# A routed expert block on one core: gate weights centred once, logits from the residual, and the rows sent in two steps

## The reference

```
x1  = x + tanh(g_xattn) * attention(ctx, ctx, layernorm(x))      # one head, width 128, per sequence of 64
n   = layernorm(x1)
logits = n @ gate_w.T                                           # 8 experts
top 2 of softmax(logits)
out = x1 + tanh(g_ffn) * sum over the 2 experts of  p * (gelu(n @ w1[e].T + b1[e]) @ w2[e].T + b2[e])
```

## Time and profile before

| | |
|---|---|
| median of 3 runs | 113.01 us (112.81 to 113.17) |
| the profiled execution: its time | 113.34 us |
| its span, first to last instruction | 111.6 us |
| mean granted TensorE clock | 0.814 |
| PE, DVE, ACT, POOL busy | 72.3, 52.6, 50.1, 53.4 us |

### The profile page before, as it was taken

One profiled execution on the slowest core, in us unless ns is written; L12 is line 12 of the kernel. 1 busy time (PEld: TensorE's weight loads), 2 busy tenths in 40 slices (PEclk: granted clock), 3 DMA queues, 4 the chain that ended last, 5 costly groups with the idle time before them and its releaser, 6 DMA issues.

```text
span 111.6 us, 2488 instructions
## 1 busy us (share of the span) xinstructions
PE 72.3 (65%) x707; PEld 61.9 (55%) x707; DVE 52.6 (47%) x222; ACT 50.1 (45%) x155; POOL 53.4 (48%) x79
## 2 busy tenths in 40 slices
PE   5667955774664200570599999999999999920000
PEld 2256823554454200210399999999999999910000
DVE  1377855499978728309812332433134213310261
ACT  4122387689676600600056654754577277600000
POOL 6668501133677777760000547454755366472050
PEclk9999999996555555569557999999999999995555
DMA  2999980000010123720553453011010111000954
GB/s 49 321 435 405 452 356 15 6 3 3 24 48 24 48 69 90 179 72 24 121 121 86 117 145 72 22 27 47 7 53 24 34 35 32 23 0 0 267 161 136
DMA packets 10748, 11.57 MB, mean 104 GB/s; under 512 B 1491, under 2 KB 9703, under 8 KB 10480
## 3 DMA queue, kind: packets, MB, share of 16 engines
q1 hardware_dynamic: 8768, 8.69, 24.3%
q0 software_dynamic: 1248, 2.12, 6.1%
q10 hardware_dynamic: 720, 0.62, 2.0%
HBM read 8.18 MB, written 3.70 MB: 106 GB/s over the span
## 4 chain that ended last, share of the span: by engine, by line
PE 37%; issue 32%; DMA 10%; POOL 7%; SPq 6%; DVE 5%
PE bank L676 18%; PE bank L664 5%; PE bank L666 5%; PE bank L665 5%; SPq L278 3%; DMA res<-results 3%; DMA wp<-in_wpack 3%; PE bank L653 3%; POOL results L391 3%; POOL x_bias L369 2%; DMA results<-y_sb,in_rows 2%; DMA in_rows<-dispatched 2%; POOL rstd L360 2%; DVE out_sb L916 1%; DVE stats L727 1%
## 5 line engine op out<-in xcount | busy, mean ns | idle before, releaser
L513 ACT ACTIVATE hid<-bank,wp 128x128 f32<-128x128 f32 x92 | 25.5, 376 | 24.7 <-PE bank L666 15.4
L391 POOL DMA_INDIRECT results<-y_sb,in_rows x23 | 22.6, 983 | 28.5 <-DVE y_sb L899 25.6
L676 PE MATMUL bank<-w_sb,hid 128*128 x184 | 25.4, 282 | 0.0
L676 PEld LDWEIGHTS bank<-w_sb,hid 128*128 128x128 f32 x184 | 22.5, 192 | 0.1
L324 POOL DMA_INDIRECT dispatched<-rows,slot x16 | 15.8, 987 | 5.1 <-issue 4.2
L664 PE MATMUL bank<-xs_t,w_hi 128*128 128x128 f16 x92 | 18.1, 231 | 0.1
L665 PE MATMUL bank<-xs_t,w_hi 128*128 128x128 f16 x92 | 18.2, 231 | 0.0
L666 PE MATMUL bank<-xs_t,w_lo 128*128 128x128 f16 x92 | 18.2, 231 | 0.0
L895 DVE COPY xs_t<-bank 128x256 f16<-128x256 f16 x23 | 6.6, 289 | 18.0 <-PE bank L653 13.2
L899 DVE TENSOR_SCALAR y_sb<-bank,in_rows 128x128 f32<-128x128 f32 x23 | 8.0, 349 | 12.9 <-PE bank L676 10.6
L522 PE MATMUL bank<-ones 128*128 128x512 bf16 x14 | 6.3, 627 | 8.9 <-issue 7.7
(11 more groups left out here) (132 smaller groups left out, 120.5 us busy)
## 6 DMA issues: line engine op xcount, KB each, us to landing
w_sb<-in_w SPq DMA_DIRECT2D x2, 2048.0 KB, 11.5
in_rows<-dispatched SPq DMA_DIRECT2D x23, 65.0 KB, 2.0
res<-results SPq DMA_DIRECT2D x4, 256.0 KB, 3.7
ctx_sb<-in_ctx_t SPq DMA_DIRECT2D x1, 512.0 KB, 5.5
out<-out_sb SPq DMA_DIRECT2D x4, 128.0 KB, 1.8
results<-y_sb,in_rows POOLq DMA_INDIRECT x23
wp<-in_wpack ACTq DMA_DIRECT2D x1, 342.0 KB, 3.8
dispatched<-pad_rows SPq DMA_DIRECT2D x5, 65.0 KB, 5.2
```

Source lines behind the costliest of these rows:

```text
L391: pool.indirect_dma_start(results_dram, bass.IndirectOffsetOnAxis(ap=in_rows[:].bitcast(U32)[:, t, TARGET:TARGET + 1], axis=0), y_sb[:, t, ...
L513: mm = act.activation(hid[:, t % HIDS, b, :], hid_ps[t % HID_PS][:, b * P:(b + 1) * P], ACT.Gelu_apprx_tanh, bias=b1[:, bass.ds(experts[t] ...
L676: mm = pe.matmul(to, hid[:, t % HIDS, b, :], w2_sb[:, bass.ds(e, 1), b * P:(b + 1) * P], start=False, stop=b == BLOCKS - 1)
```

## The change

Six things are changed at once.

1. The gate weights are centred in place of the rows: PE multiplies them once by the matrix 1/128 − identity (`mean_out`), beside the other weight products. Logits then come from the turned `neg_x1` itself (X1_T, COPY_X1_T, ROUTE), without a mean or rstd2; rstd2 goes into the scale of EXP_LOGITS (one instruction for each tile). The scaling of the logits in CHOOSE goes. The statistics are a step of their own (STATS) behind RESIDUAL.
2. The output bias goes into the values: a matmul of the identity with the bias, 512 columns in fp32, at the end of each VALUES. POOL's `x_bias` goes; RESIDUAL subtracts x itself.
3. Regions are added in RANKS, by a matmul of ones with a row of regions; both tiles of a group share matmuls. RANKS has 3, 5, 7 and 9 matmuls for groups 0 to 3, where it had 3, 7, 11 and 15. The `place` sum and the cast to `slot` go.
4. SEND becomes SEND_FIRST (2 DMAs, first expert's rows; waits for LOW) and SEND_SECOND (2 DMAs; waits for TWICE).
5. The order is planned anew: a due time for every step and group. On POOL: RSTD2 0, first 0, RSTD2 1, second 0, first 1, RSTD2 2, second 1, RSTD2 3, first 2, second 2, first 3, second 3. On PE the start is NORM_T 0, QUERIES 0, NORM_T 1, SCORES 0, VALUES 0, PROBS_T 0, QUERIES 1, ATTEND 0, SCORES 1, NORM_T 2, X1_T 0, VALUES 1, ROUTE 0, PROBS_T 1, QUERIES 2, NORM_T 3, RANKS 0 (before: VALUES 0, NORM_T 0, NORM_T 1, QUERIES 0, VALUES 1, SCORES 0, ...). On DVE: MAXIMUM 0, NUMBERS, RESIDUAL 0, STATS 0, MAXIMUM 1, LOW 0, CHOOSE 0, FILL 0, RESIDUAL 1, ... (before: ... CHOOSE 0, MAXIMUM 3, LOW 0, RESIDUAL 2, FILL 0). On ACT the first two W1_HIGH (halves of w1) stand between COPY_QUERIES 1 and COPY_X1_T 0.
6. `AHEAD` is 4, not 8: SP reads 4 row addresses before it waits for the sends, not 8.

```diff
-AHEAD = 8
+AHEAD = 4
...
-TIMES = [-1.2, -0.2, 2.2, 3.0, 4.0, 5.8, 5.2, 5.0, 7.2, 6.9, 9.2, 9.0,
-         10.7, 10.8, 10.9, 11.7, 11.1, 14.4, 14.9, 15.5, 13.6, 15.7, 15.8, 15.9]
-OFFSETS = [0, 2.7, 6.0, 8.7]
...
+TIMES = {
+    ATTEND: [14.4, 21.9, 28.8, 31.1],
...
+    FILL: [22.0, 28.5, 35.4, 38.8],
...
+    SEND_FIRST: [23.2, 29.6, 36.7, 41.8],
+    SEND_SECOND: [26.7, 33.2, 39.2, 44.3],
...
-        def send(pool, g):
+        def send(pool, g, k):
             pool.wait_ge(row_ok, g + 1)
-            pool.wait_ge(twice_ok, g + 1)
+            if k == 0:
+                pool.wait_ge(lo_ok, g + 1)
+            else:
+                pool.wait_ge(twice_ok, g + 1)
             for t in tiles_of(g):
-                for k in range(TOP_K):
-                    j = TOP_K * t + k
-                    pool.indirect_dma_start(rows_dram, bass.IndirectOffsetOnAxis(ap=slot[:, j:j + 1], axis=0),
-                                            rows[:, t, k, :], None).then_inc(sent, 16)
+                pool.indirect_dma_start(rows_dram, bass.IndirectOffsetOnAxis(ap=slot[:, t, k:k + 1], axis=0),
+                                        rows[:, t, k, :], None).then_inc(sent, 16)
...
-            pool.wait_ge(bias_ok, 1)
-            pool.tensor_tensor(x_bias[:], out_bias[:, None, :].to_broadcast((P, TILES, P)), x_sb[:], ALU.subtract).then_inc(xbias_ok, 1)
...
+                act.wait_ge(rstd2_ok, g + 1)
+                for t in tiles_of(g):
+                    m = act.activation(exps[:, t, :], shifted[:, t, :], ACT.Exp, scale=rstd2[:, t:t + 1])
...
+            pe.wait_ge(mean_set, 1)
+            pe.matmul(ps[:, 3 * P + 1:3 * P + 1 + EXPERTS], mean_out[:], wp[:, GATEW:GATEW + EXPERTS], start=True, stop=True).then_inc(fused_ps, 1)
...
+                if h == 0:
+                    pe.wait_ge(bias_ok, 1)
+                pe.matmul(v_bank[h][:, :], ident[:], out_bias[:, None, :].to_broadcast((P, HALF, P)), start=False, stop=True).then_inc(v_ps, 1)
...
+            def x1_turn(g):
+                pe.wait_ge(x1_ok, STARTS[g + 1])
...
+                    mm = pe.transpose(turn[g % 2][:, j * P:(j + 1) * P], neg_x1[:, STARTS[g] + j, :], ident[:])
...
+                pe.matmul(into(0), before[:], chosen[:, group(g), :], start=True, stop=False)
+                mm = pe.matmul(into(0), ones[:], region_row[:, 0:n, :], start=False, stop=n == 1 and g == 0)
+                for u in range(STARTS[g]):
+                    mm = pe.matmul(into(0), ones[:], counted(u, 0), start=False, stop=n == 1 and u == STARTS[g] - 1)
+                for j in range(1, n):
+                    mm = pe.matmul(into(j), ones[:], counted(STARTS[g] + j - 1, j), start=False, stop=j == n - 1)
...
-                n = then(v.tensor_tensor(logits[:, group(g), :], turn[g % 2][:, LOGIT:LOGIT + SIZES[g] * EXPERTS].rearrange(
-                    "p (j e) -> p j e", j=SIZES[g]), rstd2[:, group(g), None].to_broadcast((P, SIZES[g], EXPERTS)), ALU.mult))
...
-                n = then(v.tensor_reduce(slot_f[:, group(g), :], place_k[:, group(g), :, :], AX_X, ALU.add))
-                v.wait_ge(dve, n)
-                v.tensor_copy(slot[:, TOP_K * STARTS[g]:TOP_K * STARTS[g + 1]],
-                              slot_f[:, group(g), :].rearrange("p t k -> p (t k)")).then_inc(row_ok, 1)
+                v.tensor_tensor(place_k[:, group(g), :, :], choice[:, group(g), :, :],
+                                ranked[:, :, None, :].to_broadcast((P, SIZES[g], TOP_K, EXPERTS)), ALU.mult).then_inc(placed, 1)
+                v.wait_ge(placed, g + 1)
...
+                    v.tensor_reduce(slot[:, group(g), :], place_k[:, group(g), :, :], AX_X, ALU.add).then_inc(row_ok, 1)
```

More of the change, by code:

```diff
@@ L73 @@
[L73 to L76, removed]
+(NORM_T, COPY_NORM_T, QUERIES, COPY_QUERIES, SCORES, MAXIMUM, EXPONENT, PROBS_T, COPY_PROBS_T, ATTEND,
+ RESIDUAL, X1_T, COPY_X1_T, STATS, RSTD2, CENTRE, ROUTE, CHOOSE, EXP_LOGITS, RANKS, HIGH, LOW, FILL, TWICE,
+ SEND_FIRST, SEND_SECOND, VALUES, COPY_VALUES, W1_HIGH, NUMBERS) = range(30)
@@ new lines @@
+TIMES = {
+    ATTEND: [14.4, 21.9, 28.8, 31.1],
+    CENTRE: [17.4, 25.7, 31.5, 35.6],
+    CHOOSE: [20.1, 26.6, 32.8, 36.4],
+    COPY_NORM_T: [8.2, 10.0, 19.5, 22.4],
+    COPY_PROBS_T: [13.9, 20.5, 28.3, 30.6],
+    COPY_QUERIES: [9.4, 14.4, 21.9, 23.8],
+    COPY_VALUES: [13.3, 20.9],
+    COPY_X1_T: [17.0, 25.3, 31.2, 34.5],
+    EXPONENT: [11.7, 18.8, 26.4, 29.3],
+    EXP_LOGITS: [21.5, 27.9, 34.1, 37.8],
+    FILL: [22.0, 28.5, 35.4, 38.8],
+    HIGH: [18.1, 27.1, 33.3, 36.8],
+    LOW: [18.9, 27.9, 34.1, 37.7],
+    MAXIMUM: [11.0, 16.9, 24.6, 25.3],
+    NORM_T: [7.5, 9.3, 15.6, 21.0],
+    NUMBERS: [11.6],
+    PROBS_T: [13.2, 19.9, 27.2, 30.1],
+    QUERIES: [8.7, 13.7, 20.4, 23.0],
+    RANKS: [21.6, 27.9, 34.1, 37.8],
+    RESIDUAL: [15.3, 23.0, 29.7, 32.0],
+    ROUTE: [19.3, 25.8, 31.8, 35.0],
+    RSTD2: [17.0, 25.7, 32.2, 35.7],
+    SCORES: [10.0, 15.1, 22.6, 24.8],
+    SEND_FIRST: [23.2, 29.6, 36.7, 41.8],
+    SEND_SECOND: [26.7, 33.2, 39.2, 44.3],
+    STATS: [16.1, 23.9, 30.5, 34.7],
+    TWICE: [19.8, 28.7, 34.9, 38.4],
+    VALUES: [10.5, 16.6],
+    W1_HIGH: [14.9, 16.0, 22.8, 24.3],
+    X1_T: [16.2, 24.0, 30.6, 32.9],
+}
@@ L78 @@
+ORDER = [(step, g) for _, step, g in sorted((TIMES[step][g], step, g) for step in TIMES for g in range(len(TIMES[step])))]
 WQ, WK, WV, WOT, GATEW, BQ, BV, BO, GX, GF, B1 = 0, P, 2 * P, 3 * P, 4 * P, 4 * P + 8, 4 * P + 9, 4 * P + 10, 5 * P + 10, 5 * P + 11, 5 * P + 12
@@ L132, in gated_block @@
         out_bias = sb("out_bias", [P, P], F32)
-        x_bias = sb("x_bias", [P, TILES, P], F32)
         stats = sb("stats", [P, TILES, 6], F32)
@@ L384, in _ @@
                     rstd_of(g)
-                elif step == SEND:
-                    send(pool, g)
+                elif step == SEND_FIRST:
+                    send(pool, g, 0)
+                elif step == SEND_SECOND:
+                    send(pool, g, 1)
             pool.engine_nop().then_inc(issued, 1)
@@ L485, in _ @@
                     centre(g)
-                elif step == COPY_CENTRED_T:
-                    copy_ct(g)
+                elif step == COPY_X1_T:
+                    copy_x1t(g)
                 elif step == HIGH:
@@ L634, in _ @@
                     attend(g)
-                elif step == CENTRED_T:
-                    centred_turn(g)
+                elif step == X1_T:
+                    x1_turn(g)
                 elif step == ROUTE:
@@ L847, in _ @@
                     residual(g)
+                elif step == STATS:
+                    statistics(g)
                 elif step == CHOOSE:
```

110 lines of the change are left out of this document (54 added, 56 removed).

## The result

The changed kernel takes **110.05 us** (median of 4 runs, 109.51 to 110.33); the kernel before, run on the same chip, 112.91 us (112.62 to 113.17). The ratio is 0.9742, 95% interval 0.9696 to 0.9787: 2.9 us, 2.6% faster. The profiled execution took 109.98 us, its span is 108.2 us. Some executions of a kernel take over 1.5% longer than its fastest one with nothing changed; the ratios here leave them out, the medians and the ranges don't.

What follows compares the result with a forecast made beforehand. No engine was busy throughout; the first stage ends 21.4 us after POOL's first send starts, then a fixed hand-over. 113.34 − 3.5 = 109.8 us profiled, with the median 0.33 lower: 109.5 us; range 108.3 to 111.5.

Steps and rivals of the forecast that it cites:

- First send at 22.7: POOL's first indirect DMA would start at 22.7 us, 5.9 us earlier than 28.63, with 1.2 us to either side.
- VALUES 0 runs 11.1 to 13.4: On PE, VALUES 0 with the bias matmul would run 11.1 to 13.4 us, PROBS_T 0 following at 13.4 instead of 15.02.
- rival 4: TensorE never gets full clock in the attention stage: 114.5 us; one switch late (15.4) costs only 1.3; chance 0.04.
- The greater part of the 5.9 us is the order: The first send's 5.9 us gain would come mostly from the new step order; removed instructions give 0.6 us.
- The four `xn` at 0.3 each once L369 is gone: DVE's four normalising instructions take 0.3 us each, not 0.78, without POOL's L369; otherwise group 0 comes 1.9 us later.
- Three RSTD2 among the sends at 0.99: On POOL, three RSTD2 instead of one lie among the 16 sends, each costing 0.99 us.
- Rows of groups 1 to 3 in time, 0.4 us of waits: Later groups' slots would come just before POOL wants them, cover 0.3, 0.3 and 1.3 us; waits 0.4, bounds 0 and 2.
- rival 1: Later groups' slots come late for POOL: last send at 47.5 to 49, time 110.5 to 112.0; chance 0.13.
- Counts and padding at 41.0; SP's stretch of 9.0 us hidden or not: First padding DMA at 41.0 instead of 43.12; SP's 9.0 us to its first load taken as some 6 and hidden.
- rival 2: SP becomes the bound, first load at 50.0 and first hidden matmul at 52.7: 110.6 us, up to 111.3; chance 0.10.
- 4.7 us of half clock move with the work: The hidden layer's 4.7 us at half clock, half of it lost, would move along with the earlier work.
- rival 3: Clock switch does not move with the work: staying gives 111.3 us (chance 0.07); coming sooner, 107.2 to 108.5 (0.06).

Runs made afterwards that it cites:

- run 11: The kernel before with group 0's steps moved ahead and its sends in two steps, none of the arithmetic edits: 113.19 us, ratio to before 1.0021.
- run 5: The changed kernel with POOL's bias-minus-x instruction (L369) put back, writing to a spare tile nobody reads: 109.59 us.
- run 1: The changed kernel with two more RSTD2-like pairs of instructions on POOL behind SEND_FIRST of group 1: 111.38 us, ratio to before 0.9893.
- run 10: The changed kernel with the output bias added by VectorE as it copies the values out, instead of the bias matmul: 108.47 us, ratio to before 0.9618.
- run 12: The changed kernel with the bias added by VectorE, and 20 large matmuls on ones instead of 8 in the wait for rows: 106.99 us, ratio to before 0.9474.
- run 8: The changed kernel with AHEAD back at 8 instead of 4: 110.49 us.
- run 2: The changed kernel with all 4 sends of a group in one step at SEND_FIRST's place: 113.77 us, ratio to before 1.0123.
- run 4: The changed kernel with the bias added by VectorE in the copy of the values, instead of the bias matmul: 108.40 us, ratio to before 0.9596.

## Why the prediction was right, point by point

*Forecast 109.5 us, range 108.3 to 111.5; measured 110.05.* The mechanism was the one forecast: the end follows from the start of the first send, the roots among the sends and a fixed hand-over. Some of the signs that I gave lie just outside their bands all the same: the first send at 24.13 (21.5 to 24), the last send's end at 47.60 (45.7 to 47.3). That the time is as near as 0.5 us is partly luck: the error at the first send is 1.4 us, and two errors the other way, 0.4 and 0.6 us, took most of it back.

*First send at 22.7.* 24.13 in the profile: the one term that was mis-sized, by 1.4 us. The step was "VALUES 0 runs 11.1 to 13.4". It began at 11.09 and PROBS_T 0 at 14.66, 1.3 later than forecast, and RESIDUAL 0 came at 16.65 instead of 15.2. I took 2.3 us for VALUES 0 and the bias matmul together, 0.9 of it for the latter, where at half clock my own figures were 2.05 and 1.9, because I let the full clock come at 12 as in the one trace I had. It came at 15.3, and they cost 2.08 and 1.92. Under rival 4 the prediction has the price of that, "one switch late (15.4) costs only 1.3", but it isn't in the forecast. The table bears it out: with the rise at 12.4 to 12.6 PROBS_T 0 starts at 13.5 to 13.6 and the send at 22.9 to 23.0, near the forecast; with it at 13.8, 23.7; at 14.6 to 15.5, 24.1 to 24.4 (the kernels with the bias on PE and divided sends). Behind RESIDUAL 0 the sum held, 7.48 us to the first send where I had 7.5: the 1.37 us that FILL 0 waits for EXP_LOGITS, which I had not seen, was made up elsewhere.

*The greater part of the 5.9 us is the order.* Too simple. From PROBS_T 0 to the first send it takes 13.6 us before, 11.4 in run 11 and 9.5 in the changed kernel: 2.2 us are the order of group 0 and the split, 1.9 the arithmetic and the order around it together, and at most 1.5 (15.02 to 13.5) the new start, if the clock comes early. And run 11 shows that the first of these alone is worth nothing at the end. No run takes the arithmetic of edits 1 and 3 out of the changed kernel, so what it is worth by itself, and which of its parts, stays open.

*The four `xn` at 0.3 each once L369 is gone.* 1.11 us for four. Right, and run 5 shows the cause; the "0.78 each" was a mean of one that waited and three that didn't; but the upper bound of 1.9 us that I put on it was wrong, since `xn` has cover under VALUES 0.

*Three RSTD2 among the sends at 0.99.* 0.98; run 1 shows it with two more.

*Rows of groups 1 to 3 in time, 0.4 us of waits.* None: POOL's gaps are all 0.30, so rival 1 didn't come. With a first send 1.4 us earlier the cover would have been less, and in run 10 it shows: 0.8 us of waits.

*Counts and padding at 41.0; SP's stretch of 9.0 us hidden or not.* First padding DMA at 40.5, issues 1.90 us, and SP waits for the sends: rival 2 didn't come. I had worked the counts out from 0.19 us for each of 17 matmuls. That was a wrong reading: 0.19 was the 4.44 us from the first matmul to the counts, divided by 23, and the matmuls are not what fills that time. In the trace before all 23 start within 0.6 us (37.59 to 38.19); DVE then stood waiting, 1.2 us for the ranks and 1.36 for the counts. In the changed kernel the 17 start within 0.5 us (37.75 to 38.20), DVE doesn't wait, and the 1.69 us to the counts (39.44) are its own work on `rows` and `slot`. In run 11 the same 23 matmuls as before have 1.74 us to the counts (38.72 to 40.46). The counts came 2.6 us earlier, and none of that is shown to be the change's: the first of these matmuls starts no earlier (37.75, before 37.59), and the two waits that are gone, 2.6 us together, are gone in run 11 too, which has the old arithmetic. SP's slow stretch had a price before as well: its first load came 2.11 us after the last send, and 1.48 in the changed kernel and in run 11. It lay under `w1_lo`.

*Hand-over of 5.15.* 5.14.

*4.7 us of half clock move with the work.* They did not: 3.55 us, worth 0.6 us. This is a small part of rival 3's early half, and it paid back some of the late first send. Over the table the stretch is 2.9 to 6.0 us whatever the kernel does before, and 0 where PE was given work (12).

*The sum.* 109.8 + 1.4 (first send) − 0.4 (waits) − 0.6 (half clock) = 110.2 for a profiled execution; it took 109.98.

*`AHEAD`.* Forecast at nothing; run 8 can't tell it from nothing, nor does its profile show a wait for it.

## What to carry to other kernels

Where one engine's chain of equal steps sets the end, as the 16 sends here, the time is the start of the chain plus everything that stands between its links. An earlier start bought by moving other work in between, or by starving the later links, gives the gain back (runs 2 and 11). Work moved to TensorE before its clock has risen costs double (1.92 instead of 1.02 us): runs 4 and 10 show that the bias is better added in the copy of the result, here by moving that copy to VectorE. And a clock that falls in an idle stretch costs most in the dense stage behind it, so matmuls on ones belong right up to the end of the wait (run 12, 1.5 us). A mean over unlike instructions, or over a stretch in which the engine may be waiting, is no price of one: both 0.78 and 0.19 in the prediction were such means.
